# Layer 0's softmax on one Trainium2 core: on odd units the exponential reads the scores per head, with the maximum as its bias

## The reference

```python
def _L0_xattn_ref(emb, context, Wq, Wk, Wv, Wu, bu, qn_w, qn_b, kn_w, kn_b):
    q = (emb @ Wq.T).reshape(B, SQ, N_HEADS, KQ_DIM).transpose(0, 2, 1, 3)
    k = (context @ Wk.T).reshape(B, SK, N_HEADS, KQ_DIM).transpose(0, 2, 1, 3)
    v = (context @ Wv.T).reshape(B, SK, N_HEADS, KQ_DIM).transpose(0, 2, 1, 3)
    q = _layernorm(q, qn_w, qn_b)
    k = _layernorm(k, kn_w, kn_b)
    attn = jnp.einsum('bhqd,bhkd->bhqk', q, k) * scale
    attn = jax.nn.softmax(attn, axis=-1)
    out = jnp.einsum('bhqk,bhkd->bhqd', attn, v)
    return out.transpose(0, 2, 1, 3).reshape(B, SQ, N_HEADS * KQ_DIM) @ Wu.T + bu
x = x + jnp.tanh(g_xattn[0]) * _L0_xattn_ref(_layernorm(x), ctx_1024, ...)
x = x + jnp.tanh(g_ffn[0]) * _L0_ffn_ref(_layernorm(x), ...)
```

## Time and profile before

| | us |
|---|---|
| median of 3 runs | 1545.33 (1544.09 to 1546.13) |
| the profiled execution, whole time | 1546.16 |
| its span from first to last instruction | 1544.4 |
| outside the span | 1.8 |

### The profile page before, as it was taken

How to read it: one execution, slowest core, us unless ns; L and a number is a source line. 1 busy time by engine, 2 the same in 40 slices (tenths; PEclk the granted TensorE clock), 3 DMA queues, 4 the chain that set the end, 5 groups by cost and what they waited for, 6 DMA issues and landing times.

```text
span 1544.4 us, 26110 instructions
## 1 busy us (share of the span) xinstructions
PE 1411.3 (91%) x8820; PEld 1130.1 (73%) x8820; DVE 817.1 (53%) x2046; ACT 763.8 (49%) x1652; POOL 124.3 (8%) x115
## 2 busy tenths in 40 slices
PE   5988999999999987899979889999999998888999
PEld 3785567777898765679948746677779887556798
DVE  5793544554434747743357735445534457476532
ACT  4752445555543454554447325455555434545453
POOL 1042000000000002000011410000000100020000
PEclk9999999999999999999989999999999999999999
DMA  5002000000002000000000020000000020000000
GB/s 198 1 2 110 0 1 1 1 1 1 1 1 82 29 1 1 5 1 15 1 17 1 1 110 1 0 1 1 1 1 1 1 110 1 1 1 1 1 8 8
DMA packets 4038, 27.88 MB, mean 18 GB/s; under 512 B 1055, under 2 KB 1345, under 8 KB 2881
## 3 DMA queue, kind: packets, MB, share of 16 engines
q1 hardware_dynamic: 3040, 21.50, 3.6%
q10 hardware_dynamic: 864, 4.64, 0.8%
HBM read 25.09 MB, written 1.05 MB: 17 GB/s over the span
## 4 chain that ended last, share of the span: by engine, by line
issue 68%; PE 19%; DVE 7%; POOL 3%; ACT 2%; DMA 0%; DVEq 0%; SPq 0%; POOLq 0%; ACTq 0%
PE psum L658 17%; DVE nmax L1341 2%; POOL rs L1199 1%; PE psum L680 1%; DVE rsum L1350 1%; POOL arenaD L1212 1%; ACT arenaB L988 1%; POOL x L1224 1%; DVE arenaA L1561 1%; ACT arenaA L988 1%; DVE xn L1296 1%; DVE psum L1337 0%; DMA mask<-in_mask_dram 0%; DVE x L1373 0%; ACT probs L988 0%
## 5 line engine op out<-in xcount | busy, mean ns | idle before, releaser
L658 PEld LDWEIGHTS psum<-moe,arenaA 128*128 128x128 f32 x2048 | 239.1, 194 | 8.1 <-issue 1.9
L658 PE MATMUL psum<-moe,arenaA 128*128 128x128 f32 x2048 | 241.4, 277 | 2.2 <-DVE gt L1443 1.4
L988 ACT ACTIVATE arenaB<-psum 128x512 f32<-128x512 f32 x448 | 170.1, 432 | 147.0 <-PE psum L680 146.9
L988 ACT ACTIVATE probs<-psum,nmax 128x589 f32<-128x589 f32 (+1 forms) x256 | 125.9, 555 | 162.8 <-DVE nmax L1417 157.2
L988 ACT ACTIVATE arenaA<-psum,vec 128x512 f32<-128x512 f32 (+1 forms) x208 | 125.5, 615 | 157.2 <-PE psum L658 156.8
L658 PE MATMUL psum<-arenaD,arenaB 128*128 128x128 f32 (+2 forms) x1440 | 188.5, 279 | 10.7 <-ACT arenaB L988 9.8
L1417 DVE TENSOR_REDUCE nmax<-psum 128x1 f32<-128x589 f32 x128 | 98.7, 771 | 174.8 <-PE psum L658 174.6
L658 PEld LDWEIGHTS psum<-arenaD,arenaB 128*128 128x128 f32 (+1 forms) x1440 | 173.4, 193 | 22.1 <-issue 10.9
L1398 DVE SCALAR_TENSOR_TENSOR x<-psum,gt,x 128x128 f32<-128x128 f32 x256 | 72.1, 345 | 213.8 <-PE psum L658 213.8
L658 PE MATMUL psum<-parts 128*128 128x512 f32 x672 | 166.9, 398 | 0.0
L680 PE MATMUL psum<-w_first,probs 128*128 128x128 f32 (+2 forms) x1120 | 159.4, 273 | 3.2 <-ACT arenaA L988 3.1
(11 more groups left out here) (198 smaller groups left out, 1853.6 us busy)
## 6 DMA issues: line engine op xcount, KB each, us to landing
moe<-in_w_moe_dram SPq DMA_DIRECT2D x4, 4096.0 KB, 13.3
moe<-in_w_folds_dram SPq DMA_DIRECT2D x2, 1024.0 KB, 9.0
w_l<-in_w_l_dram ACTq DMA_DIRECT2D x1, 1372.0 KB, 12.3
x<-in_x_dram SPq DMA_DIRECT2D x4, 256.0 KB, 3.9
w_l<-in_w_l_dram ACTq DMA_DIRECT2D x1, 1024.0 KB, 9.5
out_dram<-x SPq DMA_DIRECT2D x4, 256.0 KB, 2.1
w_rest<-in_w_rest_dram ACTq DMA_DIRECT2D x1, 768.0 KB, 7.1
w_first<-in_w_first_dram ACTq DMA_DIRECT2D x1, 596.0 KB, 5.4
```

Of the source, the lines that this page charges most:

```text
L658: return nc.tensor.matmul(out, lhsT, rhs, start=start, stop=stop, skip_group_check=shared)
L988: return nc.scalar.activation(out, in_, func, **kw)
```

## The change

`by_head` now holds for layer 0 as well, on odd k: eight units of each round, sixteen in all. There VectorE leaves the subtraction out, ScalarE takes eight exponentials of 77 columns from the PSUM slot in place of one of 616 columns from SBUF, and slot S1 is given back by the last of them. VectorE's sum over the exponentials waits for that same mark, since there is no separate one. TensorE's wait ahead of the transposes stays the one for the probabilities that GpSimd has multiplied.

```diff
         def by_head(l, k):
-            return l == 6 and k % 2 == 1
+            return l in (0, 6) and k % 2 == 1
 ...
             def turn_probs(l, s, hf, t, k, r, i):
-                if by_head(l, k):
+                if l and by_head(l, k):
                     read(i, "sc", l, s, hf, t)
 ...
             def normalise(l, s, hf, t, k):
-                dve.wait_ge(*exp_ready.at(l, s, hf, t))
+                dve.wait_ge(*(reader_did("sc", l, s, hf, t) if by_head(l, k) else exp_ready.at(l, s, hf, t)))
```

## The result

| | before | changed |
|---|---|---|
| median, us | 1545.33 (1544.09 to 1546.13, 5 runs) | 1558.82 (1553.79 to 1564.45, 5 runs) |
| the profiled execution | 1546.16 | 1564.45 |
| its span | 1544.4 | 1562.3 |

The ratio is 1.0085, with a 95% interval of 1.0058 to 1.0111: slower by 13.5 us at the medians, where 12.0 was forecast. The time outside the span is 2.1 us in each of the five runs, 0.3 more than before.

What follows compares the result with a forecast made beforehand. TensorE was taken to bound the steady part, VectorE nearly so. Per round 1.85 + 4.56 - 1.50 + 1.08 = 6.0 us, 12.0 for both, gave 1557.3 us from the median; range 1550 to 1561.

Steps and rivals of the forecast that it cites:

- The bound: Layer 0's steady part: TensorE sets the pace, VectorE nearly so, so dropping the subtraction buys nothing there.
- The period: Layer 0's steady part: mixes 6.60 us apart in place of 5.46, 1.14 us more for every two units.
- The idle bracket: TensorE idle about 1.1 us ahead of every odd unit's scores, released by ScalarE's probs.
- TensorE's busy share: Layer 0's steady part: TensorE's busy time falls to about 6.7 of 8 us, VectorE's below 6.
- First mix: Start of the stage: first mix at 83.46 in place of 81.61, +1.85 us.
- Four periods: From the mix of step 5 to that of step 13: 4 x 1.14 = +4.56 us.
- xn: End of the stage: TensorE gets xn sooner, -1.5 us.
- Unit 15: End of the stage: its exponential holds up ScalarE's list 1.68 us in place of 0.60, +1.08 us on the path.
- The price of an instruction with a bias column: Eight exponentials: 2.10 us by the skill page, giving 1561; the forecast took the trace's 1.84 us.
- The rival of the queue alone: Steady part: ScalarE's list delays odd copies, slot no limit; mixes 6.1 us apart, whole 1552; chance 0.08.
- The clock: TensorE's falls to 1.2 GHz, kept as they are; all vanishing gives 1551 (rival, chance 0.10), two more 1561.

Runs made afterwards that it cites:

- The even units: Against the changed kernel, per-head exponentials on even units 4 to 14 of layer 0 instead of the odd ones: 1543.35 us, run again in more rounds 1541.82 us.
- The run with six exponentials: Kernel before, VectorE copying odd units' raw scores out of the slot, ScalarE taking six exponentials in SBUF, two over head pairs: 1556.25 us, ratio 1.0073.

## Why the prediction was right

**The bound.** It read the earlier trace rows as TensorE's pace with VectorE close behind. The even units confirm it: with VectorE's subtraction gone and no wait added, the period is still 5.46 us.

**The period.** The chain was forecast as 3.55 + 1.89 + 1.16 = 6.60 us and measured as 3.51 + 1.98 + 1.13 = 6.62 (95.36, 98.87, 100.85, 101.98), in both rounds. The idle bracket was put at about 1.1 us and reads 0.96, since the end of the transposes' records reaches into it; the shift of the scores from +4.41 to +5.49 is 1.08. TensorE's busy share was put at about 6.7 of 8 us and reads 6.94, VectorE's below 6 and reads 5.46.

**Start and end.** First mix: +1.85 forecast, 10.75 less 8.98 = +1.77 measured. Four periods: +4.56 forecast, 26.49 less 21.84 = +4.65 measured. xn: -1.5 forecast, 8.64 less 10.17 = -1.53 measured. Unit 15: +1.08 forecast, 3.12 less 2.00 = +1.12 measured. Their sum is 6.01 us a round, where 6.0 was forecast.

**The price of an instruction with a bias column.** The Trainium skill ("ScalarE: Activation LUTs", What ACT_TABLE_LOAD costs) gave the estimate of 2.10 us for eight. From the slot they take 1.83 us, as the earlier trace rows had it; from SBUF they take 2.10 in the run in which VectorE gives the slot back. So the Trainium skill's price fits there, and for PSUM it is too high by 0.27; the forecast did well to go by the row of the same source.

**The rival of the queue alone** was sized at 6.1 us a period. The run with six exponentials measured 6.12. It was a real chain, hidden behind the longer one.

**The clock** is where the forecast was weak. It kept the falls as they were, and in the profiled pair they are not. The two stretches of layer 0 are 6.51 and 6.56 us longer (59.02 to 65.53, and 58.33 to 64.89), 13.1 together, but the spans differ by 17.9. The other 4.8 stand where no instruction was changed: from the last mix of the first round to the scores of unit 2 in the second it is 703.6 us before and 711.1 after, ahead of the first stretch and behind the second it is 2.7 less. TensorE by windows (length, busy, granted clock), first before, then the changed kernel:

```profile
550.00:560.00 10.00, 7.81 (x38) 0.97 0.00 0
560.00:570.00 10.00, 9.66 (x38) 0.86 0.00 1
570.00:580.00 10.00, 8.98 (x34) 1.00 0.01 2
```

```profile
550.00:560.00 10.00, 9.29 (x40) 0.56 0.00 0
560.00:570.00 10.00, 8.95 (x23) 0.58 0.00 0
570.00:580.00 10.00, 9.14 (x29) 0.66 0.00 0
```

The changed kernel runs at 1.2 GHz for some 24 of these 30 us (mean clocks 0.56, 0.58 and 0.66). The fall begins at a group of ten matmuls behind a short wait. The same group, in the kernel before, in the changed kernel, and in the second round of the second run with the eight on the even units:

```profile
545.98 1.33 PE L658 MATMUL psum<-arenaD,arenaB 128*128 128x72 f32 x10 [0.33 <-ACT arenaB L988]
551.21 2.38 PE L658 MATMUL psum<-arenaD,arenaB 128*128 128x72 f32 x10 [0.34 <-ACT arenaB L988]
1302.25 2.40 PE L658 MATMUL psum<-arenaD,arenaB 128*128 128x72 f32 x10 [0.33 <-ACT arenaB L988]
```

In that last run the clock reads 0.61, 0.53 and 0.66 over 1300 to 1330. In both kernels VectorE's rows from about 25 us behind the start of the fall on come 8.4 us later after it than the same rows in the kernel before. The changed kernel's own second round and the other kernel's first do not have this fall. So it is not what the change does to the steady part or the end: it is one event of 8.4 us that an execution has or has not, at the same place of unchanged code, and each of these two profiles comes from the slowest run of its kernel. The other runs have no trace here, but their spans go with the mean clock: 1551.6 us at 0.985, 1557.6 at 0.981, 1562.3 at 0.978 for the changed kernel, and 1540.2 at 0.983 to 1547.5 at 0.978 for the kernel before. So a part of the 13.5 us at the medians may be the draw of the clock, of either sign, and that 13.5 lies so near to 12.0 is in part luck; that the terms of layer 0 add up to 12.0 is not. Of the first stretch's 6.51 us, 0.5 is the clock too: the fall behind xn costs 1.0 less than before, and a new one, during the mix at 127.07 (3.79 us where its twin in the earlier trace rows takes 2.50), 1.5 more. Why the clock falls in one execution and not in the next isn't settled by these runs.

## What to carry to other kernels

Moving work to an engine that is half idle is free only if it fits between that engine's own waits: look up what stands ahead of it in that engine's list, what slot it keeps, and when the next user asks. Here eight instructions with the same duration cost 1.16 us a period on odd units and nothing on even ones, where they fall into ScalarE's wait for TensorE. When a kernel spreads, look at which of its runs the profile shows, and compare the stretch that was changed before the whole. When one chain is cut, look at what ends next: without the slot 0.66 of the 1.16 us stayed.

## What was not expected of the hardware

Eight exponentials of 77 columns with a column of SBUF as bias take 1.83 us from PSUM into SBUF and 2.10 where source and result are the same tile in SBUF, start to next start 1.66 and 2.00. Whether the source alone makes the difference was not tried. The pair of copies right behind the eight from PSUM prints 0.83 us where such a pair otherwise prints 0.76.

A kernel can spread by 10.7 us over five runs, its spans in the order of their mean clocks, where the kernel before spread by 2.0 in its first five runs and by 9.3 over 25. Five runs don't tell a kernel's spread. One fall of TensorE's clock in unchanged code cost 8.4 us, more than half of what the change cost.
